# Zero products ahead of the first transposes, two later starts for GpSimd's splits, and two reorderings near the end of a two-layer gated attention kernel

## The reference, cut to what matters

```
x = x + tanh(g_xattn[0]) * L0_xattn(layernorm(x), ctx, mask, bias, weights)   # 32 heads of 128
x = x + tanh(g_ffn[0])   * L0_ffn(layernorm(x))      # one 512x512 product, 4-bit weights
x = x + tanh(g_xattn[1]) * L1_xattn(layernorm(x), ctx)   # one head of 512
x = x + tanh(g_ffn[1])   * L1_ffn(layernorm(x))      # 512x512 base product and 8 adapters of rank 16
```

## Time and profile before

| | us |
|---|---|
| median of 3 runs | 1011.15 (1010.93 to 1012.07) |
| profiled execution, its own time | 1008.72 |
| span of that execution, first to last instruction | 1006.9 |
| TensorE busy in it | 991.5 (98%) |
| VectorE, ScalarE, GpSimd busy | 472.8, 413.6, 337.8 |

### The profile page before, as it was taken

How to read it: one execution, slowest core, us unless ns; L and a number is a source line. 1 busy time by engine, 2 the same in 40 slices (tenths; PEclk the granted TensorE clock), 3 DMA queues, 4 the chain that set the end, 5 groups by cost and what they waited for, 6 DMA issues and landing times.

```text
span 1006.9 us, 14845 instructions
## 1 busy us (share of the span) xinstructions
PE 991.5 (98%) x5168; PEld 840.5 (83%) x5168; DVE 472.8 (47%) x956; ACT 413.6 (41%) x1110; POOL 337.8 (34%) x317
## 2 busy tenths in 40 slices
PE   7999999999999999999999999999999999999998
PEld 5888888888888888888888888888888887888886
DVE  4674712462155305532364235622472287666664
ACT  6554333432453244334442354234423354555640
POOL 3351314113330424041414051314131424587640
PEclk9999999999999999999999999999999999999999
DMA  8022011102110201010101010101101103210002
GB/s 311 21 85 55 26 59 61 35 12 72 42 52 0 83 24 59 10 62 21 62 31 62 21 62 31 48 35 62 31 21 63 42 1 107 113 33 2 1 1 84
DMA packets 16402, 50.52 MB, mean 50 GB/s; under 512 B 3056, under 2 KB 3312, under 8 KB 15600
## 3 DMA queue, kind: packets, MB, share of 16 engines
q1 hardware_dynamic: 15360, 48.75, 14.2%
q10 hardware_dynamic: 1008, 1.32, 0.4%
HBM read 47.97 MB, written 2.10 MB: 50 GB/s over the span
## 4 chain that ended last, share of the span: by engine, by line
PE 94%; DVE 2%; issue 1%; POOL 1%; ACT 1%; DMA 1%; SPq 0%; ACTq 0%; DVEq 0%
PE bank L1282 34%; PE bank L1340 17%; PE bank L1294 17%; PE bank L1401 9%; PE bank L1324 6%; PE bank L1304 6%; PE bank L1315 3%; PE bank L1394 2%; PE bank L1478 1%; PE bank L1498 1%; PE bank L1541 1%; DMA craw<-in_ctx 1%; POOL wvo L361 1%; DVE xt L878 0%; DVE rinv L918 0%
## 5 line engine op out<-in xcount | busy, mean ns | idle before, releaser
L1282 PE MATMUL bank<-xt,wq 128*128 128x512 f32 x768 | 186.4, 393 | 0.0
L1282 PE MATMUL bank<-ct,wk 128*128 128x512 f32 x768 | 181.6, 392 | 1.3 <-DVE ct L844 1.3
L1340 PE MATMUL bank<-wvo,ao 128*128 128x512 f32 x768 | 180.6, 392 | 0.0
L1294 PE MATMUL bank<-wvo,ct 128*128 128x512 f32 x768 | 178.0, 390 | 0.2 <-POOL wvo L361 0.2
L1294 PEld LDWEIGHTS bank<-wvo,ct 128*128 128x128 f32 x768 | 143.5, 188 | 29.8 <-POOL wvo L361 0.6
L1282 PEld LDWEIGHTS bank<-ct,wk 128*128 128x128 f32 x768 | 142.7, 188 | 30.5 <-DVE ct L844 1.9
L1282 PEld LDWEIGHTS bank<-xt,wq 128*128 128x128 f32 x768 | 142.4, 188 | 29.1
L1340 PEld LDWEIGHTS bank<-wvo,ao 128*128 128x128 f32 x768 | 142.4, 188 | 28.6
L361 POOL TENSOR_TENSOR wk<-stage,wk 128x512 fp32r<-128x512 f32 x32 | 42.3, 1321 | 296.9 <-ACT wk L542 296.9
L361 POOL TENSOR_TENSOR wvo<-stage,wvo 128x512 fp32r<-128x512 f32 x64 | 81.8, 1305 | 162.3 <-ACT wvo L542 162.3
L558 ACT ACTIVATE prob<-prob,nmax 128x128 f32<-128x128 f32 x256 | 99.3, 390 | 59.9 <-DVE nmax L909 59.9
(11 more groups left out here) (145 smaller groups left out, 1117.6 us busy)
## 6 DMA issues: line engine op xcount, KB each, us to landing
stage<-in_w SPq DMA_DIRECT2D x63, 512.0 KB, 3.3
xraw<-in_x SPq DMA_DIRECT2D x2, 1024.0 KB, 11.9
bias<-in_bias SPq DMA_DIRECT2D x8, 256.0 KB, 2.6
cs<-in_ctx SPq DMA_DIRECT2D x1, 2048.0 KB, 7.6
out<-acc SPq DMA_DIRECT2D x8, 256.0 KB, 2.2
craw<-in_ctx ACTq DMA_DIRECT2D x4, 256.0 KB, 5.8
craw<-in_ctx SPq DMA_DIRECT2D x4, 256.0 KB, 6.4
stage<-in_w_key SPq DMA_DIRECT2D x1, 1024.0 KB, 4.7
```

What stands on the lines that cost most here:

```text
L1282: mm = pe.matmul(bank[un_of[first][u] % RING][:, :], w[:, i, c, :], t[:, j, c, half(s)], start=(c == 0 and i + j == 0), stop=(c == KC - 1 ...
L1294: mm = pe.matmul(bank[un_of[first][u] % RING][:, :], ct[:, i, c, b * P:(b + 1) * P], wvo[:, j, c, :], start=(c == 0 and i + j == 0), stop= ...
L1340: mm = pe.matmul(bank[to][:, :], ao[:, h, i, b * P:(b + 1) * P], wvo[:, j, h, :], start=(h == heads[0] and i + j == 0), stop=(h == heads[- ...
```

## The change

Four edits. VectorE's first instruction clears a part of `qt`; TensorE no longer waits first for `ident` but for that, multiplies the zeros ten times into a bank that is free until tile 7, then waits for `ident`, and makes two more such products behind each of the first four turned tiles. In group 0 GpSimd waits, after the splits of `k1` and `q1`, until both halves of head 0's probabilities are scaled; its bias and mask tile and the split of `k2` come ahead of those of `o0` to `o3`, and ScalarE makes the high parts of `o0` to `o3` in head 1 instead of ahead of head 0's exponentials. Behind group 7 GpSimd waits for the last scaled probabilities before it splits the key and feed-forward weights. In the last step `adapters(q)` is cut in two, with `lo(6, 2)` between the halves for `q` = 0, and TensorE does `experts(4)` to `experts(6)` ahead of `base(7)`.

```diff
+                def rest(g, first=False):
+                    w_lo(g, "k1", first)
+                    w_lo(g, "q1", first)
+                    if first:
+                        pool.wait_ge(s_p, 2)
+                        biasmask(g, 1)
+                        w_lo(g, "k2", first)
+                    for j in range(GH):
+                        w_lo(g, f"o{j}", first)
+                    if not first:
+                        biasmask(g, 1)
+                        w_lo(g, "k2")
+                    w_lo(g, "q2", first)
...
+                pool.wait_ge(s_p, GROUPS * 2 * GH)
                 for c in range(KC):
                     split_lo("key", c)
...
                         w_hi(g, "q1", first)
-                        for j in range(GH):
-                            w_hi(g, f"o{j}", first)
                         exps(g, 0, range(2))
...
+                        if first and h == 1:
+                            for j in range(GH):
+                                w_hi(g, f"o{j}", first)
...
+                dve.memset(qt[:, 0:P], 0.0).then_inc(s_warm, 1)
...
                 lo(5, 2)
+                remaining(0)
+                lo(6, 2)
                 adapters(0)
-                lo(6, 2)
                 lo(7, 2)
...
-                pe.wait_ge(s_ident, 16)
+                pe.wait_ge(s_warm, 1)
...
+                def warm(n):
+                    for _ in range(n):
+                        pe.matmul(bank[7][:, 0:P], qt[:, 0:P], qt[:, 0:P], start=True, stop=True)
+
+                warm(10)
+                pe.wait_ge(s_ident, 16)
                 for b in range(6):
                     context_transposed(b)
+                    if b < 4:
+                        warm(2)
...
                 weighted_turned(1)
+                for u in range(HB, B - 1):
+                    experts(u)
                 base(7)
-                for u in HALVES[1]:
-                    experts(u)
+                experts(7)
```

More of the change, by code:

```diff
@@ L37 @@
 SPLITS_LOOP = CHUNKS
-SPLITS_FIRST = ["k0", "v0", "v1", "v2", "v3", "q0"] + CHUNKS[6:]
+SPLITS_FIRST = ["k0", "v0", "v1", "v2", "v3", "q0", "k1", "q1", "k2", "o0", "o1", "o2", "o3", "q2", "k3", "q3"]
 SLOTS = 8
@@ L199, in build @@
         s_g = sem("pool_prep")
+        s_warm = sem("zeros_in")
         s_cT = sem("ctx_transposed")
@@ L369, in biasmask @@
                                        bias[:, h:h + 1, :].to_broadcast([P, B, P]), ALU.add).then_inc(s_bm, 1)
[L371 to L377, removed]
+                def rest(g, first=False):
[11 more added lines that the diff above has]
+                    w_lo(g, "q2", first)
                     biasmask(g, 2)
-                    w_lo(g, "k3")
-                    w_lo(g, "q3")
+                    w_lo(g, "k3", first)
+                    w_lo(g, "q3", first)
                     biasmask(g, 3)
@@ L397, in _ @@
                 biasmask(0, 0)
-                rest(0)
+                rest(0, True)
                 def group(g):
@@ L1106, in largest, with remaining @@
                         dve.max(top8[:, u, :], rt[:, 1, u, :]).then_inc(S["top"], 1)
-                def adapters(q):
+                def remaining(q):
                     us = part(q)
@@ L1115, in adapters @@
                     dve.tensor_tensor(rt[:, 2, us, :], rt[:, 1, us, :], rt[:, 3, us, :], ALU.subtract).then_inc(S["router"], 1)
+                def adapters(q):
+                    us = part(q)
                     dve.wait_ge(S["router"], 9 * q + 7)
@@ L1223, in _ @@
                 largest(1)
+                remaining(1)
                 adapters(1)
```

## The result

The changed kernel takes 1004.47 us (median of 5, 1004.23 to 1004.65) against 1010.93 for the kernel before, run beside it (median of 5, 1008.53 to 1012.07): ratio 0.9944, 95% interval 0.9934 to 0.9955. So there are two questions: which 4.2 us went from trace to trace, and where the other 2.2 of the median come from. The spread points at an answer to the second, which the experiments then test: the runs of the kernel before lie 3.5 us apart, those of the changed one 0.4.

What follows compares the result with a forecast made beforehand. TensorE, busy 98% of the span, was taken to bound the kernel, the rest being a handful of gaps. Terms: -1.3 - 2.5 - 0.8 + 0.9 + 0.2 = -3.5 us, so 1011.15 - 3.5 = 1007.6; range 1006.9 to 1008.4.

Steps and rivals of the forecast that it cites:

- group 0: First softmax: with GpSimd held until VectorE's scalings are done, TensorE's turning loses its extra wait; gain 1.3 us.
- group 7's wait: Last softmax: turning took 3.34 us instead of 0.80 beside GpSimd's key splits; holding GpSimd gains 2.5 us.
- the low part of tile 6: Last step: VectorE makes it earlier, so TensorE's seventh adapter product no longer waits; gain 0.8 us.
- the new wait behind the last turning: Last step, second half: experts(4) now needs ScalarE's copy at once, which base(7) hid before; 0.93 us lost.
- nothing late elsewhere: After group 7: key splits keep 10.8 us margin, SP's later loads cost nothing, bank waits taken as 0, at worst 1.7.
- I carry the difference over to the median unchanged.: Whole kernel: the median, 1011.15, lay 2.4 us above the profiled execution, 1008.72; the same offset was kept after the change.
- the fall at the end of the kernel: After the last product TensorE's clock fell within about 2.3 us; used to lean to low level after 2.4 idle at start.
- The ten products of zeros ... take 2.1 us.: Start: zeros run at low level from about 1.1 to 3.2, then TensorE idles 2.4 us; term 0.2 us lost.
- the lock moves: Rival, chance 0.10: deferred splits block row scalings and bias tile 2 the second softmax; 1.7 + 0.5 given back, 1009.8.

## Why the prediction was wrong

The direction and the terms away from the start were right, and in size: group 0 (1.27 for 1.3), group 7's wait (2.55 for 2.5), the low part of tile 6 (0.89 for 0.8), the new wait behind the last turning (0.93 for 0.9), and nothing late elsewhere (key product, banks, SP's loads). Two steps failed.

*"I carry the difference over to the median unchanged."* This was the large one. The profiled execution lay 2.4 us below the median, and I had no explanation for it and looked for none. It was one of those at full clock; the median run is, by its time, one in which TensorE's clock falls to 1.2 GHz at the end of the 2.3 us wait of group 7 and costs 1.6 (by trace) to 1.9 us (1010.49 less 1008.58, the medians of the two groups of eight) more. Over the three sets 25 of 47 runs of the kernel before had the mean of 0.998, 7 of 11 with the zeros only, 7 of 12 with group 7 undone, none of 51 in the kernels in which the wait was gone or filled. The removal of a wait was worth the wait and the fall that it set off. The sign was in front of me: I used the fall at the end of the kernel (2.3 us after the last product) to argue about the start, and did not apply it to an idle stretch of the same 2.3 us at 844.9. The term should have been 2.5 and, in half of the executions, 1.6 to 1.9 more. No rival of the forecast named this.

*"The ten products of zeros ... take 2.1 us."* Each such product is two instructions. The page says so for L1304, x512 for 256 products, and the earlier trace rows for L1541, x8 for four; I read the 0.213 per instruction as one per product. With 3.9 to 4.6 us of work instead of 2.1 the clock is high by the end of the first tile in six of the nine traces with ten zeros, and there the projection starts at 10.71 to 11.26; in the other three the whole first tile runs low, and it starts at 11.44 to 11.59. Without zeros it started at 11.13 to 11.62 in four traces. The term was 0.2 lost. It measured 0.44 gained from trace to trace, but 0.03 on the kernel before (11.44 for 11.47, and nothing within 1 us in the medians) and 0.11 on the changed one (11.03 for 11.14). So a gain of some tenths in part of the executions is likely, and its mean is not told from the scatter.

Together: 4.2 from trace to trace, 1.6 to 1.9 for the clock's fall, and some 0.5 of differences between small samples make the 6.5. The rival *the lock moves* was right in that it moved (2.54 us, 1.17 us) and wrong in that it mattered. What stays open is the scatter of single runs: the runs without zeros lie 1.3 us apart and 0.8 to 0.9 higher, though the one traced, the fastest of them, starts its projection only 0.1 later, and some undone edits measured 0.5 more or less than their traces. The start alone moves by up to 0.9 us between executions (10.71 to 11.59 with ten zeros), and the sets ran on different chips. Why the clock falls in half of the executions and not in the others is open too.

## What to carry to other kernels

A profile is one execution; if its own time stands off the median, ask which kind of execution it was before carrying a sum over, and look at the mean granted clock of every run. A TensorE wait of some 2 us in a full kernel can cost nearly twice its length in a share of the runs (here 2.5 and then 1.6 to 1.9 more); so shorten such waits first, or fill them with products that nobody needs. Let GpSimd wait until VectorE's work with both inputs in SBUF is through, if it has slack, and count the instructions in the trace, not the products in the program, when costing fp32 products.

## What the runs showed of the hardware that was not expected

TensorE's granted clock fell to half in the middle of a kernel busy at 98%, right behind 2.3 us of idle time, in both executions traced for it; by the mean clock it did so in 25 of 47, and in none of 5 of the kernel that has only the 1.2 us wait of group 0. With the wait of 2.3 us filled by 20 small instructions it fell in none of 11. Transposes alone did bring the clock up: in the earlier trace rows they go from one per 0.213 us to one per 0.109 with nothing else having run. The moment differs: in the run without zeros all 24 transposes, 5.4 us of them, were still at the low level, and the projection behind them, six products in 1.62 us, was at the high one.
